# Two layers on one core: key rows by transposes, bias gradients in pairs, gate transposition three tiles later

## The reference

```python
xn = layernorm(x)
x = x + L0_attn(xn) + L0_ffn(xn)        # test-time training, 16 heads; 16 experts that choose 32 tokens each
xn = layernorm(x)
x = x + L1_attn(xn) + L1_ffn(xn)        # softmax attention, 16 heads of 8; 4 rounds of 4 experts, top 2
# L0_attn, per head, over chunks of 64 tokens, state W (64 x 64) and b:
Z1 = xk @ W + b;  x_hat = (Z1 - mean) / std;  grad_output = g * x_hat + be - (xv - xk)
grad_x = (64 * gxh - sum(gxh) - x_hat * sum(gxh * x_hat)) / (64 * std)     # gxh = grad_output * g
W = W - (eta * xk).T @ grad_x;  b = b - sum(eta * grad_x)
out = xq + g * normalised(xq @ W + b) + be                                # with the new W and b
# L1_ffn, per round r: gates = softmax of the two largest of flat @ Wg[r]
cur = cur + sum_e gates[e] * (gelu(cur @ W1[e] + b1[e]) @ W2[e] + b2[e])
```

## Time and profile before

| | us |
|---|---|
| median of the timed runs | 1176.6 (1174.9 to 1176.84) |
| profiled execution | 1178.7 |
| its span, first to last instruction | 1176.9 |
| first layer's steps, about | 44 to 412 |
| second layer's rounds, about | 490 to 1177 |
| PE busy | 1054.1 (90%) |
| DVE busy | 707.0 (60%) |
| ACT busy | 595.1 (51%) |
| POOL busy | 230.7 (20%) |

### The profile page before, as it was taken

One profiled execution on the slowest core, in us unless ns is written; L12 is line 12 of the kernel. 1 busy time (PEld: TensorE's weight loads), 2 busy tenths in 40 slices (PEclk: granted clock), 3 DMA queues, 4 the chain that ended last, 5 costly groups with the idle time before them and its releaser, 6 DMA issues.

```text
span 1176.9 us, 15629 instructions
## 1 busy us (share of the span) xinstructions
PE 1054.1 (90%) x6128; PEld 630.9 (54%) x6128; DVE 707.0 (60%) x1179; ACT 595.1 (51%) x870; POOL 230.7 (20%) x183
## 2 busy tenths in 40 slices
PE   2786999999999898499999899999999999899997
PEld 1464777777776667345444544544544444544453
DVE  7777887788788544746545545644544653554462
ACT  3443554555454252255556556555556555555652
POOL 6454555565565001300000000000000000000000
PEclk9887999999999799699999999999999999999999
DMA  7000000000000021000001001100101000110110
GB/s 208 1 1 1 1 1 1 1 1 1 2 1 1 1 72 46 27 36 37 5 32 36 37 9 37 36 1 37 46 1 36 37 36 1 45 37 1 36 37 9
DMA packets 16936, 29.28 MB, mean 25 GB/s; under 512 B 5624, under 2 KB 11532, under 8 KB 14816
## 3 DMA queue, kind: packets, MB, share of 16 engines
q1 hardware_dynamic: 15232, 26.02, 6.8%
q10 hardware_dynamic: 1632, 2.27, 0.6%
HBM read 27.11 MB, written 1.18 MB: 24 GB/s over the span
## 4 chain that ended last, share of the span: by engine, by line
PE 71%; DVE 19%; ACT 6%; issue 2%; POOL 1%; DMA 0%; SPq 0%; POOLq 0%; DVEq 0%; ACTq 0%
PE bank L1344 17%; PE bank L1008 8%; DVE mx L866 6%; PE bank L1010 5%; PE bank L1009 5%; PE quad L1047 5%; PE bank L1261 4%; PE bank L1152 3%; ACT ex L565 3%; PE quad L1310 3%; PE quad L1127 2%; PE bank L1115 2%; PE quad L1300 2%; PE quad L1044 2%; ACT hd L550 2%
## 5 line engine op out<-in xcount | busy, mean ns | idle before, releaser
L1344 PE MATMUL bank<-hd,W 128*128 128x512 f32 x512 | 244.5, 605 | 0.0
L550 ACT ACTIVATE hd<-bank,b1c 128x512 f32<-128x512 f32 x256 | 176.1, 688 | 104.6 <-PE bank L1010 101.7
L866 DVE TENSOR_REDUCE mx<-quad 128x4 f32<-128x2048 f32 x64 | 146.4, 2288 | 60.6 <-PE quad L1300 60.6
L872 DVE SCALAR_TENSOR_TENSOR add<-bank,b2T,cwB 128x512 f32<-128x512 f32 x64 | 48.0, 751 | 201.7 <-PE bank L1344 201.7
L565 ACT ACTIVATE ex<-quad 128x2048 f32<-128x2048 f32 x64 | 120.1, 1877 | 94.1 <-PE quad L1310 94.1
L1344 PEld LDWEIGHTS bank<-hd,W 128*128 128x128 f32 x512 | 90.6, 189 | 116.3 <-issue 97.0
L1008 PE MATMUL bank<-cH,W1h 128*128 128x512 f32 x192 | 86.2, 449 | 5.6 <-DVE cL L883 2.7
L1009 PE MATMUL bank<-cH,W1l 128*128 128x512 f32 x192 | 75.9, 395 | 0.0
L1010 PE MATMUL bank<-cL,W1h 128*128 128x512 f32 x192 | 75.9, 395 | 0.0
L1047 PE MATMUL quad<-Wbd,arena 128*64 128x128 f32 x1024 | 73.9, 289 | 0.0
L1261 PE MATMUL bank<-ex,Vx 128*32 128x512 f32 x512 | 68.2, 605 | 0.0
(11 more groups left out here) (277 smaller groups left out, 2016.7 us busy)
## 6 DMA issues: line engine op xcount, KB each, us to landing
cwB<-gate_rows SPq DMA_DIRECT2D x16, 1024.0 KB, 4.7
ex<-in_L_ffn_W SPq DMA_DIRECT2D x1, 1024.0 KB, 5.5
out<-fin SPq DMA_DIRECT2D x4, 256.0 KB, 2.3
x<-in_L_attn_hidden_states SPq DMA_DIRECT2D x2, 256.0 KB, 4.1
x<-in_L_attn_hidden_states ACTq DMA_DIRECT2D x2, 256.0 KB, 5.3
arena<-in_L_attn_wk SPq DMA_DIRECT2D x1, 512.0 KB, 7.1
arena<-in_L_attn_theta ACTq DMA_DIRECT2D x1, 512.0 KB, 7.2
arena<-in_L_attn_wv ACTq DMA_DIRECT2D x1, 512.0 KB, 8.7
```

What stands on the lines that cost most here:

```text
L550: act.activation(hd[:, n, :], bank[4 + n % 2][:, :], ACT.Gelu_apprx_tanh, bias=b1c[:, n:n + 1]).then_inc(ROUND["gelu_ready"], 1)
L866: dve.tensor_reduce(mx[:, t, :], quad[:, :, :], AX_X, ALU.max, negate=True).then_inc(ROUND["score_max"], 1)
L872: dve.scalar_tensor_tensor(out=add[:, e % 2, :], in0=bank[4 if e % 2 else 6][:, :], scalar=b2T[:, e:e + 1], in1=cwB[:, e, :], op0=ALU.add, ...
L1344: last = pe.matmul(bank[4 if e % 2 else 6][:, :], W2[:, e, a, :], hd[:, n, :], start=(a == 0), stop=(a == NF - 1))
```

## The change

In the first layer:

- PE: `XK_` transposes four blocks of `kT` instead of projecting. `Z` and `Zq` become `state`: both bias rows first, then both products. `bias` runs every second step and sums the gradients of two slots with two matmuls into neighbouring 32-row parts of `db_`. It stands behind `dW`. `queries` stands before `turn`, with `att` right behind `turn`.
- ACT: `bias_high` copies 36 rows every second step. `squares_q` stands before `deviation`, `deviation_q` before `take_xk`, `take_queries` before `take_turned`.
- DVE: `bias_low` runs every second step over 36 rows, with a multiplication and an addition in one instruction. `rdev_q` and `normed` belong to the same step and stand between `gradient` and `sum_gx_xhat`. The parts of `choice` are called in steps 0 to 3 (two, two, two, one) instead of 0 to 4 (two, one, one, one, two).

In the second layer, `turn_gates` stands behind tile 7 instead of tile 4, and ACT's copy of the gates behind its gelu 7.

```diff
             for s in range(4 * NC + 6):
-                take_att(s - 2), squares(s), deviation(s), take_u(s), squares_q(s), take_xk(s), deviation_q(s), bias_high(s - 1)
-                take_keys(s), take_turned(s - 1), take_queries(s)
+                take_att(s - 2), squares(s), squares_q(s), deviation(s), take_u(s), deviation_q(s), take_xk(s)
+                if s % 2 == 0:
+                    bias_high(s // 2 - 1)
+                take_keys(s), take_queries(s), take_turned(s - 1)
...
-                    if n == 4:
+                    if n == 7:
                         act.wait_ge(ROUND["gates_turned"], R + 1)
...
-            def bias_low(s):
-                if s in LIVE:
-                    r = slice(32 * (s % 4), 32 * (s % 4) + 2)
-                    dve.wait_ge(CHUNK["bias_high"], s + 1)
-                    dve.tensor_tensor(Bhl[r, :], db_[r, :], Bhl[r, :], ALU.subtract).then_inc(CHUNK["bias_split"], 1)
+            def bias_low(m):
+                if 0 <= m < 2 * NC:
+                    r = slice(64 * (m % 2), 64 * (m % 2) + 36)
+                    dve.wait_ge(CHUNK["bias_high"], m + 1)
+                    dve.scalar_tensor_tensor(out=Bhl[r, :], in0=Bhl[r, :], scalar=C("low_minus")[r, :], in1=db_[r, :], op0=ALU.mult, op1=ALU.add).then_inc(CHUNK["bias_split"], 1)
...
-                normed(s - 1), bias_low(s - 2), sum_squares(s), xhat(s), sum_squares_q(s), gradient(s), sum_gx_xhat(s), rdev_q(s), update(s - 1)
+                if s % 2 == 1:
+                    bias_low((s - 3) // 2)
+                sum_squares(s), xhat(s), sum_squares_q(s), gradient(s), rdev_q(s), normed(s), sum_gx_xhat(s), update(s - 1)
                 if s == 0:
                     choice(0), choice(1)
-                elif s <= 3:
-                    choice(s + 1)
-                elif s == 4:
-                    choice(5), choice(6)
+                elif s == 1:
+                    choice(2), choice(3)
+                elif s == 2:
+                    choice(4), choice(5)
+                elif s == 3:
+                    choice(6)
...
+            def state(s):
+                i, hf = s // 4, s % 4 // 2
+                if 4 <= s < 4 * NC + 4:
+                    pe.wait_ge(CHUNK["bias_split"], s // 2 - 1)
                 if s in LIVE:
                     if s:
                         pe.wait_ge(CHUNK["xhat_ready"], s)
+                    bias_row(s, zb)
                 if s in AFTER:
                     if s > 4:
                         pe.wait_ge(CHUNK["normed_ready"], s - 4)
+                    bias_row(s, zqb)
+                if 4 <= s < 4 * NC + 4:
+                    pe.wait_ge(CHUNK["state_updated"], s - 3)
+                if s in LIVE:
+                    pe.wait_ge(CHUNK["keys_taken"], 4 * i + 2 * hf + 2)
+                    product(s, kT, zb).then_inc(CHUNK["z_ready"], 1)
+                if s in AFTER:
+                    pe.wait_ge(CHUNK["queries_taken"], 4 * (i - 1) + 2 * hf + 2)
+                    product(s, qT, zqb).then_inc(CHUNK["zq_ready"], 1)
...
-                    mm3(second_bank[:, :], two(xth, i, g), two(xtl, i, g), wkh[:, ws], wkl[:, ws]).then_inc(CHUNK["xk_ready"], 1)
+                    for a in range(4):
+                        last = pe.transpose(second_bank[:, a * P:(a + 1) * P], kT[:, 4 * hf + a, 2 * g:2 * g + 2, :].rearrange("p b c -> p (b c)"), ident)
+                    last.then_inc(CHUNK["xk_ready"], 1)
...
+            def bias(m):
+                if 0 <= m < 2 * NC:
+                    pe.wait_ge(CHUNK["grad_ready"], 2 * m + 2)
+                    for u in (2 * m % 4, 2 * m % 4 + 1):
+                        last = pe.matmul(db_[32 * u:32 * u + 32, :], C("pair_t"), gw[:, u, :], start=False, stop=True, skip_group_check=True)
+                    last.then_inc(CHUNK["bias_ready"], 1)
...
             for s in range(4 * NC + 6):
-                Z(s), target(s), Zq(s), XK_(s), bias(s - 1), dW(s - 1), keys(s), turn(s - 1), queries(s), att(s - 1)
+                state(s), target(s), XK_(s), dW(s - 1)
+                if s % 2 == 0:
+                    bias(s // 2 - 1)
+                keys(s), queries(s), turn(s - 1), att(s - 1)
...
-                hidden(4)
+                hidden(4), hidden(5), scores(1), hidden(6), hidden(7)
                 turn_gates()
-                hidden(5), scores(1), hidden(6), hidden(7), scores(2), hidden(8), hidden(9)
+                hidden(8), scores(2), hidden(9)
```

More of the change, by code:

```diff
@@ L431, in take_queries, with bias_high @@
                     act.activation(qT[:, 2 * m:2 * m + 2, :, :].rearrange("p a b c -> p (a b c)"), second_bank[:, :], ACT.Copy).then_inc(CHUNK["queries_taken"], 1)
-            def bias_high(s):
-                if s in LIVE:
-                    r = slice(32 * (s % 4), 32 * (s % 4) + 4)
-                    act.wait_ge(CHUNK["bias_ready"], s + 1)
+            def bias_high(m):
+                if 0 <= m < 2 * NC:
+                    r = slice(64 * (m % 2), 64 * (m % 2) + 36)
+                    act.wait_ge(CHUNK["bias_ready"], m + 1)
                     act.activation(Bhl[r, :], db_[r, :], ACT.Copy).then_inc(CHUNK["bias_high"], 1)
@@ L1039, in _, with bias_row, product @@
             LIVE, AFTER = range(4 * NC), range(4, 4 * NC + 4)
-            def through(s, T, to):
-                hf, g = s % 4 // 2, s % 2
+            def bias_row(s, to):
                 r = slice(32 * (s % 4), 32 * (s % 4) + 4)
                 pe.matmul(to[:, :], pair[r, :], Bhl[r, :], start=True, stop=False, skip_group_check=True)
+            def product(s, T, to):
+                hf, g = s % 4 // 2, s % 2
                 for a in range(4):
@@ L1049, in through @@
                 return last
-            def Z(s):
+            def state(s):
+                i, hf = s // 4, s % 4 // 2
+                if 4 <= s < 4 * NC + 4:
+                    pe.wait_ge(CHUNK["bias_split"], s // 2 - 1)
                 if s in LIVE:
[L1053 to L1057, removed]
                     if s:
                         pe.wait_ge(CHUNK["xhat_ready"], s)
-                    through(s, kT, zb).then_inc(CHUNK["z_ready"], 1)
-            def Zq(s):
+                    bias_row(s, zb)
                 if s in AFTER:
[L1064 to L1068, removed]
                     if s > 4:
                         pe.wait_ge(CHUNK["normed_ready"], s - 4)
-                    through(s, qT, zqb).then_inc(CHUNK["zq_ready"], 1)
+                    bias_row(s, zqb)
[7 more added lines that the diff above has]
+                    product(s, qT, zqb).then_inc(CHUNK["zq_ready"], 1)
             def target(s):
@@ L1087, in XK_ @@
                 if s in LIVE:
-                    i, hf, g = s // 4, s % 4 // 2, s % 2
-                    ws = slice(hf * 512, (hf + 1) * 512)
+                    hf, g = s % 4 // 2, s % 2
                     if s == 0:
@@ L1110, in queries, with dW @@
                     features(second_bank, (s - 2) % 4, (s - 2) // 4, wqh, wql).then_inc(CHUNK["queries_ready"], 1)
-            def bias(s):
+            def bias(m):
+                if 0 <= m < 2 * NC:
+                    pe.wait_ge(CHUNK["grad_ready"], 2 * m + 2)
+                    for u in (2 * m % 4, 2 * m % 4 + 1):
+                        last = pe.matmul(db_[32 * u:32 * u + 32, :], C("pair_t"), gw[:, u, :], start=False, stop=True, skip_group_check=True)
+                    last.then_inc(CHUNK["bias_ready"], 1)
+            def dW(s):
                 if s in LIVE:
                     pe.wait_ge(CHUNK["grad_ready"], s + 1)
-                    pe.matmul(db_[32 * (s % 4):32 * (s % 4) + 32, :], C("pair_t"), gw[:, s % 4, :], start=False, stop=True, skip_group_check=True).then_inc(CHUNK["bias_ready"], 1)
-            def dW(s):
-                if s in LIVE:
                     pe.wait_ge(CHUNK["xk_taken"], s + 1)
```

## The result

| | before | after |
|---|---|---|
| median of four runs, us | 1176.72 (1174.9 to 1181.77) | 1138.64 (1136.34 to 1140.5) |
| ratio, with its 95% interval | | 0.9669 (0.9634 to 0.9704) |
| profiled execution / its span | 1178.7 / 1176.9 | 1136.3 / 1134.5 |
| PE busy | 1054.1 (90%) | 1014.6 (89%) |

Faster by 38.1 us, against 39.6 forecast.

The account below looks back on a forecast made before the run. PE bounds the first layer; in the second only its waits for gates and maxima can be gained. First layer -6.7 and second layer -33.1 sum to -39.8 us, giving a median of 1137, range 1119 to 1150 for 8 in 10.

Parts of the forecast that it names:

- the circle: First layer: a loop of waits through several engines, from T(1) to the next T(1), sets a chunk at 40.6 us.
- the wait before attention output: First layer, PE: attention output right behind the turn waits 0.75 us for ACT's copy, twice a chunk.
- the longer gradient: First layer: `rdev_q` and `normed` ahead of `sum_gx_xhat` make dW start 11.3 us after T, against 10.4.
- DVE's loop: First layer: T to T on DVE takes 9.0 us without bias_low, 9.8 with the paired one, 18.8 for two steps.
- Steps 9 to 29: First layer's five steady chunks: 0.2 us gained in each, 1 us in all.
- PE's new gaps lower its clock: Rival, first layer: waits lower PE's clock for half its busy time, six chunks lose 90 us, 1227; chance 0.05.
- First steps: First layer up to step 9: the token choice moved to earlier steps gains 7.3 us, bounds 3 and 10.
- End: End of the first layer: bias, turn, new wait and attention output follow the last gradient in line, +1.5 us.
- Second layer: Second layer, PE: the gates' transposition three tiles later saves about 2.07 us a round, 33.1 over 16 rounds.
- DVE's pace: Rival, first layer: only DVE's 37.6 us remain for a chunk, 5 x 3.0 less, 1122; chance 0.20.
- Half of the second layer: Rival, second layer: tiles' circle through ACT is slower, so a round gains only 1.0 us, 1154; chance 0.12.
- transposes in line: Rival, first layer, PE: the key rows' new transposes do not overlap and take 1.1 us, 1141; chance 0.04.

Follow-up runs that it names:

- the experiment that shows its price (0.55): The kernel with turn ahead of queries and query state behind the target, `normed` moved from behind the gradient's last sum to ahead of it: 1131.57 us, ratio 0.9595.
- the run with 41.32: After with `rdev_q` and `normed` back behind the gradient's last sum (`sum_gx_xhat`): 1149.07 us, ratio 0.9762.
- the fastest one: After with turn ahead of queries, query state (row and product) behind the target, and `normed` behind the gradient's last sum: 1123.05 us, ratio 0.9549.

## Why the prediction was right

*PE's sum and the three reasons.* PE 36.3 predicted, 36.31 found; the circle 40.6 predicted, 40.26 found. Its members, in the prediction's order, came to 9.06, 11.32, 6.26, 4.12, 7.14 and 2.36, against 9.2, 11.3, 6.2, 4.3, 7.2 and 2.4. Of the three items that give the 4.5 us back, the first is shown by an experiment: the wait before attention output (0.75 predicted, though its pieces as written add up to 0.79; 0.74 found), whose removal gives 1.45 a chunk. The second, the longer gradient, is read in after as the member of 11.32; the experiment that shows its price (0.55) is in another order, and in after's own order taking it away made the chunk 1.1 longer. The third, DVE's loop, is read from the rows only: T(1) to T(2) takes 9.06, and the early squares of the queries, for which I had added 0.25, add nothing (1.06 from T to the reciprocal, as in before).

*Where PE stands idle.* Here the prediction had the wrong place. It named waits for the gradient before dW, up to 2.2 in step 2 and 0.8 in step 3; they are 0.5 at most, 3.6 in all between 144 and 341 us. The larger wait, 8.5 in all and 1.49 in step 2, is that of the query's state row for `normed`, which the prediction doesn't name. The chain runs through the gradient and not through this wait, so it takes up time in which PE would otherwise have stood before dW, and the sum held; that it counts as soon as `normed` is later is what the run with 41.32 shows.

*Unknown costs.* A bias pair took 0.98 (1.0 taken), new transposes 0.44 for four (0.44), the two state rows 0.66 (0.67). The Trainium skill (TensorEngine Tiling (Array Packing), Tiling Modes) says that a change of the tiling mode drains the array; the trace agrees, since the second row of the same mode adds 0.23 and one that stands alone takes 0.42. The transposes' 0.44 holds for their place behind the target; behind a product they take 0.59 in other kernels here, so the price belongs to the neighbours too.

*Steps 9 to 29.* Forecast -1.0, found +0.4. Three of the five chunks are at 40.26, 0.5 a chunk better than before; two lost 1.6 each to the clock. The rival "PE's new gaps lower its clock" was right in its mechanism and wrong in its size: I had priced half of all chunks' busy time, and what fell was the clock of one step's first matmuls. The argument against it, that waits of 2.7 left the clock at 1.00, rested on one round; another round of before shows the opposite (last section). In the timeline of PE the same wait stands ahead of both kinds (L1049 is the state row; 0.49 is its time at full clock):

```profile
191.83 0.72 PE L1049 MATMUL quad<-Bhl,pair 4*128 4x512 f32 x1 [1.49 <-DVE arena L743]
...
233.68 0.49 PE L1049 MATMUL quad<-Bhl,pair 4*128 4x512 f32 x1 [1.49 <-DVE arena L743]
```

*First steps.* -6.0 against -7.3, inside the bounds of 3 to 10; the wait of 9.25 is gone. T(5) came at 103.60 (102.7 forecast), and from there to T(9) it was 41.12 (40.7). The run with the old choice gives 5.0 of it to the choice.

*End.* This is the term that is furthest off: +1.5 taken, -2.0 found. The order of events was right, as step 33 starts 17.64 after T(31) (17.65 predicted). But I took what follows as it stood before, and before it ran at the lower clock for most of it, which I had not looked up. The stretch, and the first two rows of it, of before, and then those of after:

```profile
398.00:412.40 14.40, 10.94 (x61) 9.11 (x61) 9.39 (x16) 2.72 (x7) 0.00 (x0) 0.63 0.00 1
...
398.65 0.76 PE L1044 MATMUL quad<-Bhl,pair 4*128 4x512 f32 x1 [1.75 <-DVE arena L741]
399.33 1.98 PE L1047 MATMUL quad<-Wbd,arena 128*64 128x128 f32 x16
```

```profile
394.09 0.47 PE L1049 MATMUL quad<-Bhl,pair 4*128 4x512 f32 x1 [2.22 <-DVE arena L743]
394.49 1.09 PE L1055 MATMUL quad<-Wbd,arena 128*64 128x128 f32 x16
```

Sixteen products of the same kind take 1.98 and 1.09. Most of the -2.0 is this one execution's, and not the edits': the kernel with the gates put back has the same first layer, and there the clock fell at the same products, behind a shorter wait:

```profile
396.68 0.76 PE L1049 MATMUL quad<-Bhl,pair 4*128 4x512 f32 x1 [2.01 <-DVE arena L743]
397.37 1.98 PE L1055 MATMUL quad<-Wbd,arena 128*64 128x128 f32 x16
```

From T(31) to the first expert matmul it took 39.62, 0.8 more than before; with the key rows projected it was 40.63, with the old choice 39.83. In kernels with before's first layer the same stretch took 37.30 to 40.50. So +1.5 isn't refuted, and that after's profile shows -2.0 is luck with the clock. Why the clock held in after, no run here tells.

*Second layer.* -2.07 a round forecast, 2.02 to 2.05 found, but for two rounds (2.3 in the first, 2.7 in the one that took 45.72). The walk's times hold: scores(1) 1.6 earlier, outputs at 542.64, and the first expert waits for PE only (1.03, as in the earlier trace rows), so the spread load's slack was enough. Some 2.2 us of the -34.6 are the clock of before's one profiled execution: its last 16.9 us ran at 0.89 and are 1.6 longer than the same work in the kernel with the gates put back, and one of its batch rounds took 45.72 where the others took 45.1, with the lower clock right behind its wait for the gates.

*Rivals.* DVE's pace did not come in after. With PE's order changed a chunk of 38.5 did, on a circle that is DVE's loop for two of its steps and PE for the rest. Half of the second layer did not come either, nor transposes in line: four take 0.44 by the chain. The 275 ns of the Trainium skill (TensorE: Matmul & The Clock Gate, Part 4: PE-mode transpose) are the length of one (0.27 in the trace), and no pace of several. That 39.6 and 38.1 lie so close owes something to luck, in errors that cancel: 1.3 and 1.4 too much in the first steps and chunks, 3.5 and 1.5 too little in the end and the second layer. By those terms the span fell by 2.6 more than forecast (42.4). The median fell by 1.5 less than forecast, since before's profiled execution (1178.7) was 2.0 slower than its median and after's (1136.3) 2.3 faster: the table of stretches compares one above its median with one below.

## What to carry to other kernels

When the busiest engine is close to a circle of waits through several engines, sum that circle before pricing its work: here 4.5 us a chunk off PE gave 0.5, and the order of two items in two engines' lists gave 1.45. A term that is carried over unchanged has a clock too, so look that up, and in more than one execution. An instruction joined with another waits for both of their inputs, so look at what stands behind the later one. A wait that an in-order queue takes early, for something only needed later, is the cheapest thing to remove, and the gain is found by walking the queue instruction by instruction.

## What the runs showed of the hardware

The same wait of PE can be followed by the lower granted clock or not. One of 1.49 us, in a stretch where PE is otherwise busy for nine tenths, was followed by it in two of the five steady chunks of after, and one of about that length in three of the five with the gates put back, each time for 1.5 to 1.6 us more. Before shows it too, in the rounds that begin a batch. The wait for the gates is 2.66 in both of these, and what follows runs at full clock in one and not in the other (L1010 is the third of three like matmuls; the last line is the whole second round):

```profile
668.93 0.60 PE L1363 MATMUL bank<-cst,cw 128*4 128x128 f32 x4 [2.66 <-DVE cw L862]
...
669.85 0.40 PE L1010 MATMUL bank<-xL,W1h 128*128 128x512 f32 x1
```

```profile
837.91 0.60 PE L1363 MATMUL bank<-cst,cw 128*4 128x128 f32 x4 [2.66 <-DVE cw L862]
...
838.95 0.63 PE L1010 MATMUL bank<-xL,W1h 128*128 128x512 f32 x1
...
830.36:876.08 45.72, 42.75 (x198) 23.29 (x197) 22.47 (x37) 24.41 (x29) 0.00 (x0) 0.96 0.08 29
```

The steady chunks of kernels without such a wait in them (before, and the fastest one) never show it. With the gates moved, rounds that begin a batch took 44.6 instead of 43.0 in three of the kernels, once or twice in each, at a clock of 0.96; there PE stands 1.6 for a maximum. I can't tell from these runs what separates the cases, and so each of these kernels keeps some 2 to 5 us that no sum over rows of one execution gives.

The cost of a small group of matmuls depends on what stands before it. Four transposes take 0.44 behind the target's matmuls and 0.59 behind the product of queries and state, three matmuls of 512 columns 0.70 and 0.89 in the same two places, a bias row 0.23 behind another one and 0.42 alone.
